# Three chains in one loop pass of a vision tower with a state-space layer: one transformer layer each of two pairs, and the state space of a third

## The reference, cut to what matters

```
x = patch_embed(images)                      # 196 patches of 16x16x3 -> 128, and a class token: T = 197
for l in 0, 1:                               # 8 heads of 16
    q, k, v = split(rmsnorm(x) @ wqkv_l.T)
    x = x + softmax(q k^T / 4) v @ wo_l.T
    h = rmsnorm(x); x = x + (silu(h @ wg.T) * (h @ wu.T)) @ wd.T      # width 344
h = rmsnorm(x)
for d in forward, backward:                  # state space, 16 states, 128 channels
    xc, z = split(h @ W_in); xs = silu(conv4(xc) + b)
    dt_in, B, C = split(xs @ W_xproj)        # 32, 16, 16
    dt = softplus(dt_in @ W_dt + b_dt)
    s[t] = exp(dt * A) * s[t-1] + dt * B * xs
    y_d = ((s * C).sum over states + D * xs) * silu(z) @ W_out
h = layernorm(h + y_f + y_b)
h = layernorm(h + experts(h))                # 64 experts, top 8 of 4 groups, capacity 256 tokens each
```

## Time and profile before

| | us |
|---|---|
| median of 3 runs (12876.94 to 12912.05) | 12895.33 |
| the profiled execution: its span, and the time that it is given | 13032.3 |
| a loop pass after the routing has ended | 184.3 |

### The profile page before, as it was taken

How to read it: one execution, slowest core, us unless ns; L and a number is a source line. 1 busy time by engine, 2 the same in 40 slices (tenths; PEclk the granted TensorE clock), 3 DMA queues, 4 the chain that set the end, 5 groups by cost and what they waited for, 6 DMA issues and landing times. The chain is left out here.

```text
span 13032.3 us, 153093 instructions
## 1 busy us (share of the span) xinstructions
PE 8924.6 (68%) x48772; PEld 5897.0 (45%) x48772; DVE 8016.1 (62%) x13143; ACT 5903.0 (45%) x13164; POOL 2489.9 (19%) x1809
## 2 busy tenths in 40 slices
PE   5656566577777777777777777777777777777642
PEld 3434344344444444444444444444444444444421
DVE  3556566566666666666666666666666666666724
ACT  4334343444544454445444544445444544454411
POOL 0222222211111111111111111111111111111164
PEclk8777777787878888878878887878787878888755
DMA  2000000000000000000000000000000000000034
GB/s 88 7 11 6 12 6 8 10 10 5 10 10 10 5 10 10 10 6 9 10 10 10 5 10 10 10 5 10 10 10 5 10 10 10 6 9 10 2 53 111
DMA packets 130841, 183.68 MB, mean 14 GB/s; under 512 B 27033, under 2 KB 112893, under 8 KB 121469
## 3 DMA queue, kind: packets, MB, share of 16 engines
q1 hardware_dynamic: 95068, 150.00, 3.6%
q0 software_dynamic: 34816, 21.19, 1.2%
HBM read 113.96 MB, written 57.12 MB: 13 GB/s over the span
## 5 line engine op out<-in xcount | busy, mean ns | idle before, releaser
L478 POOL TENSOR_TENSOR hs<-hs 128x788 f32<-128x788 f32 x512 | 949.7, 1855 | 7866.3 <-DVE hs L904 7866.3
L608 ACT ACTIVATE P<-psS,least_s 99x197 f32<-99x197 f32 x4096 | 1394.7, 428 | 1437.9 <-DVE least_s L791 1437.0
L1109 PE MATMUL psS<-KM,Q 128*99 128x394 f32 x4096 | 1757.9, 549 | 162.0 <-issue 61.9
L897 DVE TENSOR_TENSOR_SCAN hs<-dA,hs 128x1576 f32<-128x1576 f32 x512 | 1763.9, 3445 | 27.5
L1123 PE MATMUL psS<-cst,P 99*99 99x99 f32 x8192 | 1108.5, 288 | 818.9 <-ACT P L608 762.8
L692 ACT ACTIVATE dA<-dt_,aneg 128x394 f32<-128x394 f32 x2048 | 1179.4, 617 | 682.5 <-DVE hs L897 682.5
L1123 PEld LDWEIGHTS psS<-cst,P 99*99 99x99 f32 x8192 | 963.7, 194 | 1133.1 <-ACT P L608 1047.3
L1219 PE MATMUL psA<-bc,bcsel_h 96*128 96x394 bf16 x2048 | 786.1, 384 | 800.4 <-DVE hs L904 624.0
L791 DVE TENSOR_REDUCE least_s<-psS 99x4 f32<-99x788 f32 x1024 | 991.2, 973 | 278.6 <-PE psS L1109 265.7
L1109 PEld LDWEIGHTS psS<-KM,Q 128*99 128x99 f32 x4096 | 729.7, 187 | 703.9 <-issue 536.0
L575 ACT ACTIVATE sq<-X 128x197 f32<-128x197 f32 x640 | 228.5, 366 | 1780.3 <-DVE X L824 1140.3
(11 more groups left out here) (203 smaller groups left out, 15631.5 us busy)
## 6 DMA issues: line engine op xcount, KB each, us to landing
pat<-patches SPq DMA_DIRECT2D x64, 1176.0 KB
rows_scratch<-zeros SPq DMA_DIRECT2D x1, 19104.0 KB, 61.9
hs<-sum_scratch SPq DMA_DIRECT2D x24, 512.0 KB, 3.5
out<-hs SPq DMA_DIRECT2D x24, 512.0 KB, 2.6
sum_scratch<-HW SPq DMA_DIRECT2D x64, 148.5 KB
slot_scratch<-toki,sloti POOLq DMA_INDIRECT x320
dA<-w SPq DMA_DIRECT2D x32, 128.0 KB
sum_scratch<-HW SPq DMA_DIRECT2D x64, 48.5 KB
```

The costliest lines, as they stand in the source:

```text
L478: nc.gpsimd.tensor_tensor(hs[:, g % HBUF, 0:2, :], hs[:, g % HBUF, 0:2, :], hs[:, g % HBUF, 2:4, :], ALU.add).then_inc(half_summed, 1)
L608: last = nc.scalar.activation(P[:, b, m, 0:T], psS[0:CT, 2 * b + m // 2, m % 2 * T:(m % 2 + 1) * T], ACT.Exp, bias=least_s[:, b, m:m + 1], ...
L897: nc.vector.tensor_tensor_scan(h, dA[:, g % 2, :, :].rearrange("p n t -> p (n t)"), h, 0.0, ALU.mult, ALU.add).then_inc(scan_ready, 1)
L1109: last = mm(psS[0:CT, 2 * b + j, 0:2 * T].rearrange("p (e t) -> p e t", e=2), Q[:, b, q * CT:(q + 1) * CT], KM[:, b, m:m + 2, 0:T], start= ...
```

## The change

- **Three chains.** A loop pass now holds layer 0 of pair k+2, layer 1 of pair k+1 and the state space of pair k. The two layers are roles r = 0 and 1, with their own tiles, semaphores and PSUM banks: psS banks 2r and 2r+1, and bank r of psG. psA is gone.
- **Merged images.** Both images of a pair go through most stages in one instruction of 394 columns. Attention runs in eight rounds of two heads (`ROUNDS = NQ * HP`); each image of each role has one bank for its scores. KM is made by ScalarE from PSUM, one copy per head with the mask column as scale.
- **B/C rows by DMA.** ScalarE copies dt_in, B and C once to SBUF (`dtbc`). SyncE stores B and C (32 x 394) to DRAM and loads four rows at a time, repeated on all 128 partitions: B straight into the state buffer `hs` (three buffers), C into `cr` (two). Each multiply of VectorE then takes four rows, 1576 columns. The splits and the selection matmuls are gone.
- **The sum over states.** VectorE adds four rows to two (`half`), TensorE accumulates both in psY with two matmuls. GpSimd keeps only the copy of H and the indirect DMAs.
- **A table of turns.** `STAGES` is one written-out list for both roles, and `PLACE` gives, for each engine, the stage behind which each unit is issued.
- The scratch tiles of the routing now lie in `dA`, `SG` lies in `cr`, and R and EF lie in `PTs`.

The diff, cut to its core:

```diff
-ROUNDS = [(q, h) for q in range(NQ) for h in range(2)]
+HP = HEADS // 2
+ROUNDS = NQ * HP
-MULS = 2 * NS * 2
+MULS = 2 * QUARTERS
 HBUF = 3
+CBUF = 2
...
+UNITS += [("decay", g, k) for g in range(2) for k in range(QN)] + [("input", 0)]
 for _g in range(QUARTERS):
+    UNITS += [("load", _g + 3)] if _g + 3 < QUARTERS else []
+    UNITS += [("scan", _g)] + ([("half", _g - 1), ("sum", _g - 1)] if _g else [])
+    UNITS += [("input", _g + 1)] if _g + 1 < QUARTERS else []
+    UNITS += [("decay", _g + 2, _k) for _k in range(QN)] if _g + 2 < QUARTERS else []
+    UNITS += [("output", _g)]
...
+PLACE = {'dve': [0, 0, 0, 1, 3, 1, 2, 5, 8, ...], 'act': [...], 'pe': [...]}
...
+            run(0, None, None)
+            run(1, 0, None)
+            run(2, 1, 0)
+            with eng.Fori(0, STEPS - 3 - peel) as i:
+                run(i + 3, i + 2, i + 1)
...
+            run(None, STEPS - 1, STEPS - 2)
+            run(None, None, STEPS - 1)
...
+            def load(i, g):            # SyncE
+                d, n = divmod(g, QUARTERS // 2)
+                if n == 0:
+                    q.wait_ge(bc_stored, i * 32 + d * 16 + 16)
+                    q.sem_inc(q_waited, 1)
+                if g >= HBUF or not is_first(i):
+                    q.wait_ge(acc_done, i * QUARTERS + g - HBUF + 1 if g >= HBUF else i * QUARTERS)
+                q.dma_start(hs[:, g % HBUF, :, :], bc_d[d:d + 1, n * QN:(n + 1) * QN, :].to_broadcast([128, QN, N])).then_inc(b_loaded[g % HBUF], 16)
+                if g >= CBUF or not is_first(i):
+                    q.wait_ge(mul_done, i * MULS + MUL_OUT[g - CBUF] if g >= CBUF else i * MULS)
+                q.dma_start(cr[:, g % CBUF, :, :], bc_d[d:d + 1, NS + n * QN:NS + (n + 1) * QN, :].to_broadcast([128, QN, N])).then_inc(c_loaded[g % CBUF], 16)
...
-                nc.gpsimd.tensor_tensor(hs[:, g % HBUF, 0:2, :], hs[:, g % HBUF, 0:2, :], hs[:, g % HBUF, 2:4, :], ALU.add).then_inc(half_summed, 1)
-                pool.wait_ge(half_summed, i * QUARTERS + g + 1)
-                nc.gpsimd.tensor_tensor(hs[:, g % HBUF, 0, :], hs[:, g % HBUF, 0, :], hs[:, g % HBUF, 1, :], ALU.add).then_inc(summed, 1)
...
+            def keys(i, r, h):         # ScalarE
+                act.wait_ge(kq_done[r], i * 2 + 1)
+                for k in (2 * h, 2 * h + 1):
+                    last = nc.scalar.activation(KM[:, r, k, :, :].rearrange("p g t -> p (g t)"), psG[:, r, 0:2 * TP], ACT.Copy, scale=c("heads", k, k + 1))
...
-                dve.wait_ge(bb_done, i * MULS + m + 1)
-                nc.vector.tensor_tensor(hs[:, g % HBUF, k, :], u[:, g // (QUARTERS // 2), :], AB[m % 2][:, 0:N], ALU.mult).then_inc(mul_done, 1)
+                nc.vector.tensor_tensor(hs[:, g % HBUF, :, :], hs[:, g % HBUF, :, :], u[:, d, :].unsqueeze(1).to_broadcast([128, QN, N]), ALU.mult).then_inc(mul_done, 1)
...
+            def half(i, g):            # VectorE
+                dve.wait_ge(mul_done, i * MULS + MUL_OUT[g])
+                nc.vector.tensor_tensor(hs[:, g % HBUF, 0:2, :], hs[:, g % HBUF, 0:2, :], hs[:, g % HBUF, 2:4, :], ALU.add).then_inc(half_summed, 1)
...
-                mm(AB[m % 2][:, 0:N], bcsel[:, row, :], bc[:, d, :], start=True, stop=True).then_inc(bb_done, 1)
```

More of the change, by code:

```diff
@@ L57 @@
-UNITS += [("decay", 0, k) for k in range(QN)]
-for _g in range(QUARTERS):
[L59 to L67, removed]
@@ L69 @@
-STAGES = [f"{n}.{b}" for n in ["conv"] + [f"{n}.{l}" for l in range(2) for n in LAYER_STAGES] + ["normf"] for b in range(G)]
-WEIGHT = {"conv": 6, "norm.0": 3, "norm.1": 3, "norm2.0": 10.2, "norm2.1": 5.22, "qkv.0": 2.5, "qkv.1": 2.88,
[3 rows of a table removed]
[L76 to L83, removed]
-        name, *layer = stage.split(".")[:-1]
-        return ".".join([name.rstrip("0123") if name != "norm2" else name] + layer)
-    w = [WEIGHT[key(n)] for n in STAGES]
-    cost = [COST[u[0].strip("-")] for u in UNITS]
-    out, acc, k, used = {}, 0, 0, 0
-    for n, x in zip(STAGES, w):
-        acc += x
-        while k < len(UNITS) and used + cost[k] / 2 <= acc / sum(w) * sum(cost):
-            used += cost[k]
-            k += 1
-        out[n] = k
-    out[STAGES[-1]] = out[STAGES[-2]] = len(UNITS)
-    return out
@@ new lines, in role_stages @@
+def role_stages(r):
+    out = [("conv", 0)] if r == 0 else []
+    out += [("square", r, 0), ("norm", r, 0), ("qkv", r), ("keys", r, 0)]
+    for n in range(ROUNDS):
+        out += [("score", r, n, b) for b in range(G)]
+        out += [("keys", r, n + 1)] if n + 1 < HP else []
+        out += [("value", r, 0)] if n == HP else []
+        out += [("turn", r, n, b) for b in range(G)]
+    out += [("value", r, 1), ("den", r), ("wo", r), ("square", r, 1), ("norm", r, 1), ("gate", r), ("sig", r), ("up", r), ("down", r)]
+    out += [("square", r, 2), ("norm", r, 2)] if r else []
+    return out
@@ L103, in _cols @@
+_muls = [u for u in UNITS if u[0] in ("input", "output")]
+MUL_IN = [_muls.index(("input", g)) + 1 for g in range(QUARTERS)]
+MUL_OUT = [_muls.index(("output", g)) + 1 for g in range(QUARTERS)]
 def _cols(widths):
@@ new lines, in _, with square @@
+            front = [chain(act, act_front[r], ACT_FRONT[r]) for r in range(2)]
+            def square(i, r, m):
+                if r and not m:
+                    act.wait_ge(xb_ready, i + 1)
+                else:
+                    act.wait_ge(x_ready[r], i * 2 + m if r else i * 3 + 2 + m)
+                nc.scalar.activation(sq[:, r, :], X[:, (r + 1 if m else r), :, :].rearrange("p g t -> p (g t)") if r else X[:, 0, :, :].rearrange("p g t -> p (g t)"), ACT.Square).then_inc(sq_ready[r], 1)
```

825 lines of the change are left out of this document (346 added, 479 removed), and 3 rows, old and new, of the table WEIGHT.

## The result

| | before | after |
|---|---|---|
| median, us | 12898.80 (4 runs) | 10565.01 (4 runs, 10562.62 to 10569.58) |
| ratio, 95% interval | | 0.8191 (0.8179 to 0.8202) |
| span of the profiled execution | 13032.3 | 10560.5 |
| a pass after the routing has ended | 184.3 | 150.2 |
| a pass that routes | 232.4 | 170.7 |

What follows compares the result with a forecast made beforehand. Two in-order chains holding each other up, not throughput, were taken as the bound. 210.6 start, 62 passes x 147 = 9114, routing 450, one pass 125, tail 724 gave 10,624, or 10,510 us in runs; range 9,450 to 11,650.

Steps and rivals of the forecast that it cites:

- TensorE was forecast at 122: TensorE's busy time per pass falls from 133.8 to 122 us at the same clock, mainly as 64 selection matmuls go.
- 139 from VectorE's density: Reading of a pass: VectorE's 114.4 us of work at the 82% density of today's second half gives 139 us.
- 155 from the overlap of chains: Reading of a pass: two layers side by side 80 us plus state space 100, times today's 0.86, gives 155 us.
- better than 0.86: Overlap factor of a pass may improve on 0.86, as its serial part falls from two layers in a row to one.
- Evenness: VectorE's busy shares in the two halves of a pass should be nearer each other than 54 and 82%.
- At least 8.0 us before it is wanted: Each B or C load is issued at least 8.0 us of VectorE work before its use; it lands in 5.4.
- Costing the loads at nothing: The 16 loads a pass, 12.9 MB, add no time, hidden by VectorE's work on the groups between.
- The selection matmuls' waits: TensorE's 15.6 us wait on multiplies before the selection matmuls loses its reason; cited for the 130 us pass.
- denser rival: Rival: the table fills VectorE to 88%, a pass is 130 us, the kernel 9470 us in runs; chance 0.20.
- the order costs what it hides: Rival: three chains in one order stall each other, pass 167 us, kernel 11,740 us in runs; chance 0.16.
- 45 us on each of 10 passes: The 10 routing passes each take 45 us extra, 450 in all, as their row of waits gets no shorter.
- the factor 0.9895: Ratio of the runs' median to the profiled execution before, used to turn the 10,624 total into 10,512 us.

Runs made afterwards that it cites:

- idle instructions at the scans: Changed kernel plus eight idle VectorE instructions a pass, one behind each scan: 11117.34 us, ratio to before 0.8645, pass 160.4 us.
- the copies added: Changed kernel with an 803 KB DRAM-to-DRAM copy ahead of each of the 16 loads of a pass: 10678.35 us, ratio to before 0.8302, pass 151.8 us.
- all three engines relieved: Changed kernel without half sums, one sum matmul per group, K copied for even heads only in the loop (result incomplete): 10096.29 us, ratio to before 0.7831.

## Why the prediction was right, and where it was not

**The pass: 147 forecast, 150.2 measured.** VectorE 114.4 against 113.5, ScalarE 91.8 against 90.2, and single prices held: wide multiply 1.79 (1.8), half sum 0.96 (0.98), least score 0.56, the upper of my two bounds (0.50 to 0.56). The K copy was mis-sized, 0.61 for 0.50. TensorE was forecast at 122 "at the same clock", and is 112.1 at 0.86 where it was 0.81; at 0.81 the same work would be some 119 (estimate, 112.1 x 0.86 / 0.81; the kernel with idle instructions at the scans has 118.3 at 0.82). The step from work to time took the middle of two readings, 139 from VectorE's density and 155 from the overlap of chains. The second is the nearer, and the experiments speak for it: work moved between engines hardly shows, and another order of the roles, under the same table, moves a pass by 61 us. That a shorter serial part makes the factor better than 0.86 fits the result (150.2 of my estimated 180, 0.83) but isn't shown by itself, since every kernel with one role at a time also lacked a table of its own. That 147 lies as near as it does is in part luck: the middle of two readings is not a mechanism, and the first reading, by VectorE's density, came out too low by 11 us.

**Evenness.** I expected VectorE's shares in the two halves nearer than 54 and 82%: they are 74 and 77%. Cut at the scans they are 90 and 52%, so an even pair of halves hides an uneven pass.

**The loads.** "At least 8.0 us before it is wanted" was wrong as a minimum: B of group 5 has 4.85, since its issue waits for TensorE's sum, which the table puts late. Costing the loads at nothing was right. By the figure of the Trainium skill, page "DMA: Bandwidth & Descriptors", section "Latency and other measured facts", I had estimated 7.2 us for a load in a busy stretch; the trace has 4.1 for B and 5.6 for C, and only with the copies added, at half of the DMA engines' time, 7.4 and 9.6.

**The selection matmuls' waits.** They are gone, and of ScalarE's wait for X, 28.1 us then, 16.1 are left. The denser rival (130 us) didn't come: even with all three engines relieved a pass is 143.4. The rival "the order costs what it hides" (167) didn't come with this table. Its mechanism, a wide instruction in front of a least score, is how I read the two-chain kernel with rows by DMA and half sums, at 211.6.

**Routing: the step that failed.** I took 45 us on each of 10 passes, "a row of waits that gets no shorter, only POOL is freer". It is 20.5. GpSimd's sums have little part in it: in two chains with rows by DMA it is 17.0 with them and 17.1 without, against 48.1 in the kernel before, and half sums put on GpSimd in the changed kernel add 5. Before, the row of routing steps hides something else. While GpSimd issues its 32 indirect DMAs (timeline of the kernel before, 1598 to 1637 us), TensorE and ScalarE both creep, with idle time that the profile calls issue. The first projection for B and C is done in time, at 1610.5. But ScalarE copies its result (`hi`, L669) only at 1642.53, behind copies for the attention that come late, and VectorE waits 33.9 us for that. Lines of TensorE, then of ScalarE:

```profile
1609.57 0.90 PE L1204 MATMUL psA<-XZ,wts 128*96 128x394 f32 x2
...
1619.57 1.21 PE L1093 MATMUL psG<-PT,V 99*32 99x99 f32 x20 [8.40 <-issue]
...
1637.44 0.33 PE L1123 MATMUL psS<-cst,P 99*99 99x99 f32 x1 [1.77 <-issue]
```
```profile
1631.12 0.83 ACT L616 ACTIVATE PT<-psS 99x792 f32<-99x792 f32 x1 [11.70 <-issue]
...
1642.53 0.49 ACT L669 ACTIVATE hi<-psA 96x394 bf16<-96x394 f32 x1
```

And the wait of VectorE in that pass:

```profile
DVE res L861 <- ACT hi L669: 36.5, 2, 33.9
```

In the changed kernel neither engine has such gaps there, nor in the two-chain kernel with rows by DMA. What starves them before is open.

**The sum.** In the profiled execution's terms 10,624 was forecast and 10,560.5 came: the start -16, 62 passes at 3 us more (+198), routing -245, the tail -12, and the two passes at the ends +12. Then the factor 0.9895 from that execution to the median failed: the profiled execution of the changed kernel lies at the median (10562.82 for 10565.01), which puts back 112. So that 10,510 comes so near to 10,565 is luck: the pass and the factor were off by +198 and +112, the routing by -245, and the small terms by -16.

## What to carry to other kernels

Where several in-order engines hand work to each other dozens of times in a pass, look at the order and at how many independent pieces are under way, not at the busy time alone: here nearly the same work took 211.6 us with two pieces, in orders not made for it, and 150.2 with four in a table that was. A part that looks like a saving (fewer instructions, less TensorE) can cost alone, as the rows by DMA did (+13.7, and +27.3 with the half sums). By my reading that is because its long instructions stand in front of short ones that another engine waits for, so give it an order made for it. Once the order is fitted, price an edit by running it: here 4.3 us less of TensorE were worth nothing, and 7.1 us more of VectorE cost 10.2 or 5.1, by their place.
